# A fused attention and LoRA kernel: first loads laid out anew, cache rows fetched by GpSimd's indirect DMA, transposed keys from step 11

## The reference, cut to what matters

```python
q = einsum('bsd,ed->bse', x, Wq)   # 32 heads of 128
k = einsum('bsd,ed->bse', x, Wk)   # 8 heads of 128
v = einsum('bsd,ed->bse', x, Wv)
q = rope(rmsnorm(q, q_norm_w), cache_seqlens + arange(128))
k = rope(rmsnorm(k, k_norm_w), cache_seqlens + arange(128))
kc = k_cache[block_table].reshape(8, 512, 8, 128)   # 16 pages of 32 rows a sequence
vc = v_cache[block_table].reshape(8, 512, 8, 128)
k_all, v_all = concatenate([kc, k]), concatenate([vc, v])
scores = where(valid, q k_all^T / sqrt(128), -1e30)
x = x + (softmax(scores) @ v_all) @ Wo^T
x = x + linear with a LoRA; x = x + linear with 8 gated LoRA experts; x = x + SwiGLU with LoRAs
```

## Time and profile before

| | |
|---|---|
| median of 3 runs | 1474.0 us (1472.37 to 1478.88) |
| the profiled execution's own time | 1474.48 us |
| its span, first to last instruction | 1472.7 us |
| mean granted TensorE clock | 0.992 |
| attention, up to its last residual addition | about 1138 us |
| PE busy in the span | 1412.7 us (96%) |
| GpSimd (POOL) busy | 792.3 us (54%) |

### The profile page before, as it was taken

One profiled execution on the slowest core, in us unless ns is written; L12 is line 12 of the kernel. 1 busy time (PEld: TensorE's weight loads), 2 busy tenths in 40 slices (PEclk: granted clock), 3 DMA queues, 4 the chain that ended last, 5 costly groups with the idle time before them and its releaser, 6 DMA issues.

```text
span 1472.7 us, 27069 instructions
## 1 busy us (share of the span) xinstructions
PE 1412.7 (96%) x8052; PEld 1216.4 (83%) x8052; DVE 1113.9 (76%) x2236; ACT 852.8 (58%) x2082; POOL 792.3 (54%) x768
## 2 busy tenths in 40 slices
PE   2899999999999999999999999999997999899999
PEld 1788888888888888888888888888885777788887
DVE  4788888888888888888888888888886555554444
ACT  1666666666666767676676766666664322433332
POOL 5555555565555666666666666665551002454342
PEclk9999999999999999999999999999999899999999
DMA  4433333333333232223222222322425500334341
GB/s 125 152 111 105 107 104 102 102 108 105 113 100 104 69 81 66 65 65 75 68 67 65 65 78 62 70 55 47 116 43 164 113 1 1 110 118 118 118 117 66
DMA packets 192562, 129.68 MB, mean 88 GB/s; under 512 B 119041, under 2 KB 159745, under 8 KB 190113
## 3 DMA queue, kind: packets, MB, share of 16 engines
q1 hardware_dynamic: 192416, 127.96, 31.8%
HBM read 125.04 MB, written 24.64 MB: 102 GB/s over the span
## 4 chain that ended last, share of the span: by engine, by line
PE 81%; SPq 11%; issue 3%; DVE 3%; POOL 1%; DMA 1%; ACT 1%; DVEq 0%; POOLq 0%
PE banks L300 19%; PE banks L301 19%; PE banks L302 19%; PE banks L1207 10%; PE banks L1184 8%; SPq L346 5%; SPq L330 2%; SPq L354 2%; PE banks L1148 2%; DMA w_raw<-in_w_att 1%; PE banks L1376 1%; PE banks L1362 1%; PE banks L1254 1%; POOL w_pair L475 1%; PE banks L1302 1%
## 5 line engine op out<-in xcount | busy, mean ns | idle before, releaser
L651 ACT ACTIVATE prob<-prob,nbias 128x640 f32<-128x640 f32 x256 | 210.2, 822 | 151.9 <-DVE nbias L837 151.9
L812 DVE TENSOR_TENSOR pt_pair<-banks,pt_pair 128x640 fp32r<-128x640 f32 x256 | 211.0, 824 | 106.1 <-ACT pt_pair L647 103.6
L837 DVE CUSTOM_DVE_ANT_0 prob<-banks,mask,q_rs 128x640 f32<-128x640 f32 x256 | 220.2, 879 | 42.4 <-PE banks L302 42.4
L1207 PE MATMUL banks<-w_pair,o_pair 128*128 128x512 f32 x768 | 224.4, 414 | 2.1 <-DVE o_pair L812 2.1
L647 ACT ACTIVATE pt_pair<-banks 128x640 fp32r<-128x640 f32 x256 | 179.5, 701 | 42.8 <-PE banks L1184 42.8
L300 PE MATMUL banks<-w_pair,x_pair 128*128 128x256 f32 (+1 forms) x512 | 179.1, 350 | 21.4 <-POOL w_pair L475 21.4
L1184 PE MATMUL banks<-ident,prob 128*128 128x128 f32 x1280 | 184.2, 274 | 4.7 <-DVE pt_pair L812 4.7
L1184 PEld LDWEIGHTS banks<-ident,prob 128*128 128x128 f32 x1280 | 146.5, 140 | 47.3 <-issue 35.4
L301 PE MATMUL banks<-w_pair,x_pair 128*128 128x256 f32 (+1 forms) x512 | 174.1, 340 | 0.0
L302 PE MATMUL banks<-w_pair,x_pair 128*128 128x256 f32 (+1 forms) x512 | 173.4, 339 | 0.0
L300 PE MATMUL banks<-kt_pair,qt_pair 128*128 128x320 f32 x512 | 164.3, 321 | 2.5 <-DVE kt_pair L812 2.2
(11 more groups left out here) (188 smaller groups left out, 3488.0 us busy)
## 6 DMA issues: line engine op xcount, KB each, us to landing
w_raw<-in_w_att SPq DMA_DIRECT2D x64, 320.0 KB, 3.1
w_raw<-in_fw SPq DMA_DIRECT2D x66, 256.0 KB, 3.4
x_raw<-in_xT SPq DMA_DIRECT2D x64, 256.0 KB, 3.2
kt_all<-in_kT SPq DMA_DIRECT2D x128, 128.0 KB, 2.5
kv_raw<-in_kv SPq DMA_DIRECT2D x416, 32.0 KB, 1.6
kt_raw<-kt_all SPq DMA_DIRECT2D x38, 256.0 KB, 3.0
kv_raw<-in_kv SPq DMA_DIRECT2D x608, 16.0 KB, 1.6
fb_all<-in_gu_b SPq DMA_DIRECT2D x32, 176.0 KB
```

Of the source, the lines that this page charges most:

```text
L651: act.activation(prob[:, h, :], prob[:, h, :], ACT.Exp, bias=nbias[:, h:h + 1], scale=-1.0, accum_out=psum_row[:, h:h + 1]).then_inc(exped, 1)
L812: dve.tensor_tensor(pair[1], src, pair[0].bitcast(F32), ALU.subtract).then_inc(lo_sem, 1)
L837: dve.tensor_tensor_reduce(out=prob[:, h, :].rearrange("p (a n) -> p a n", a=2), in0=score_ps[h % 2][:, :, 0:HALF], in1=mask[:, n % B, :]. ...
L1207: last = pe.matmul(misc_ps, o_pair[:, j, h, :], w_pair[:, k, ds(at + h * HID, HID)], start=i == 0, stop=i == 3 * REP - 1)
```

## The change: what it does

1. **First loads.** The first group's weights come from an array of their own, `w_boot`, into a buffer `boot_raw` that holds all of them, in seven DMAs with a semaphore each: K and V columns first, then q's in four, then the output projection's 1 MB. `boot_raw` lies where `pt_pair` will be. VectorE makes high and low parts of x and of the first six itself; GpSimd makes the low part of the output projection's four. `tabs` are made for one sequence at a time: sequence 0 before step 0, then `make_tabs(n + 2)` at the end of VectorE's steps 0 to 5. Four instructions are made of eight. `w_att` pieces 0 to 7 are no longer loaded.
2. **Cache rows.** GpSimd computes row numbers once, and `load_rows(n + 2)` issues four indirect DMAs a step, each of 128 rows of 1 KB (K and V together, in all 64 steps). It stands behind `v_low(n)` and ahead of `kc_low(n+1)`. SP issues no cache rows.
3. **Transposed pages.** SP gathers all 16 pages of a sequence in each of steps 0 to 7, and `BY_ROWS` is 11: cached keys come by columns from step 11 on. SP waits once for all gathers.
4. ScalarE issues the loads of the page numbers, the first rotation rows, `wnorm` and `ident` at the start. The sign of the sine moves from the table to a subtraction.

The diff, cut to its core:

```diff
-BY_ROWS = 3 * B + 2
+BY_ROWS = B + 3
 # SP
+            def load_kt(n, par):
+                if n >= BY_ROWS + 2:
+                    sp.wait_ge(kc_lo, n - BY_ROWS - 1)
+                if n == BY_ROWS:
+                    sp.wait_ge(s_gathered, 16 * NPP * B)
+                    sp.wait_ge(tab_done, B)
+                sp.dma_start(kt_raw[:, par, :]..., kt_all[n % B, :, n // B]...).then_inc(s_ktin[par], 16)
+            def gather_keys(b):
                 _, pages = nc.values_load_multi_w_load_instructions(...)
                 for j, page in enumerate(pages):
-                    a = PSIZE * (j % 4)
-                    sp.dma_start(kv_raw[a:a + PSIZE, par, j // 4, at:2 * D], t["kv"][...]).then_inc(s_kvin[par], 16)
-                if 2 <= n < BY_ROWS:
-                    gather_keys(b, pages, (n - 2) // B)
+                    sp.dma_start(kt_all[b, j]..., t["kT"][ds(page), :, :]...).then_inc(s_gathered, 16)
             load_x(0, 0)
-            load_w(0, 0)
-            load_w(1, 1)
+            for j, (lo, hi) in enumerate(BOOT_COLS):
+                sp.dma_start(boot_raw[:, lo:hi], t["w_boot"][:, lo:hi]).then_inc(s_boot[j], 16)
+            load_x(1, 1)
...
+            sp.dma_start(boot_raw[:, WWO:GW], t["w_boot"][:, WWO:GW]).then_inc(s_boot[len(BOOT_COLS)], 16)
             def step(n, par, x=True, w=True):
...
-                load_kv(n + 2, par, True)
+                if n < B:
+                    gather_keys(n)
+                if n + 2 >= BY_ROWS:
+                    load_kt(n + 2, par)
 # GpSimd
+            def load_rows(n, par):
+                if n >= 2:
+                    pool.wait_ge(v_lo, n - 1)
+                    pool.wait_ge(kt_done, n - 1)
+                for c in range(KC - 1):
+                    pool.indirect_dma_start(kv_raw[:, par, c, :], None, t["kv"],
+                                            bass.IndirectOffsetOnAxis(ap=row_at[:, n % B, c:c + 1], axis=0),
+                                            element_offset=(n // B) * PAGES * PSIZE * 2 * D).then_inc(s_kvin[par], 16)
...
                 v_low(n, par)
+                if n + 2 < NT:
+                    load_rows(n + 2, par)
                 if nxt and n + 1 >= BY_ROWS:
                     kc_low(n + 1, 1 - par)
-                if isinstance(n, int) and n == 0:
-                    w_low(PIECES - 1, 1)
                 if x:
                     x_low(n + 2, par)
                 if w:
                     w_low(n + PIECES, par)
 # VectorE, before step 0
+            def boot_split(j):
+                lo, hi = BOOT_COLS[j]
+                dve.wait_ge(s_boot[j], 16)
+                dve.tensor_scalar(w_pair[:, 0, lo:hi], boot_raw[:, lo:hi], 1.0, None, ALU.mult).then_inc(boot_hi, 1)
+                dve.wait_ge(boot_hi, j + 2)
+                dve.tensor_tensor(w_pair[:, 1, lo:hi], boot_raw[:, lo:hi], w_pair[:, 0, lo:hi].bitcast(F32),
+                                  ALU.subtract).then_inc(boot_lo, 1)
+            for j in range(len(BOOT_COLS)):
+                boot_split(j)
+            make_tabs(0)
+            dve.wait_ge(s_boot[len(BOOT_COLS)], 16)
+            for j in range(REP):
+                lo, hi = WWO + j * HID, WWO + (j + 1) * HID
+                dve.tensor_scalar(w_pair[:, 0, lo:hi], boot_raw[:, lo:hi], 1.0, None, ALU.mult).then_inc(boot_out_hi, 1)
+            q_times_cos(0)
...
+            k_rope(0, 0)
+            qt_low(0)
+            kt_low(0)
 # VectorE, end of a step
+                if n + 2 < B:
+                    make_tabs(n + 2)
 # TensorE
-            pe.wait_ge(s_const, 48)
             project_kv(0, 0)
             project_q(0, 0)
+            pe.wait_ge(s_const, 16)
```

More of the change, by code:

```diff
@@ L48 @@
 QKV_PIECES = -(-WWO // PW)
+BOOT_COLS = [(WKV, WKV + HID), (WKV + HID, WWO)] + [(j * HID, (j + 1) * HID) for j in range(DC)]
 POS_END = 1645
@@ L112, in build @@
         qt_pair = sb("qt_pair", [P, 2, REP, P], F32R, where=att)
+        boot_raw = sb("boot_raw", [P, GW], where=boot)
+        boot.close()
         pt_pair = sb("pt_pair", [P, 2, REP, KC, P], F32R, where=att)
@@ L239, in build @@
         kt_hi, kt_lo = sem("kt_hi"), sem("kt_lo")
-        s_gathered = [sem(f"s_gathered{b}") for b in range(B)]
+        s_gathered = sem("s_gathered")
+        s_page, page_step, rows_known = sem("s_page"), sem("page_step"), sem("rows_known")
         s_ktin = [sem(f"s_ktin{i}") for i in range(2)]
@@ L676, in step @@
                 pt_high(n, 2)
-            x_high(0, 0)
+            act.wait_ge(added, 1)
+            for j in range(KC - 1):
+                act.dma_start(page_i[j * PSIZE:(j + 1) * PSIZE].rearrange("p b c -> p (b c)"),
+                              t["pages_by_place"][j].partition_broadcast(PSIZE)).then_inc(s_page, 16)
+            act.dma_start(in_page[:, 0:1], t["in_page"]).then_inc(s_page, 16)
+            act.activation(spare[:, 0:1], spare[:, 2:3], ACT.Copy)
+            _, first_length = nc.values_load_multi_w_load_instructions(
+                t["seqlens"].unsqueeze(0)[:, 0:1], engines=[act.engine], min_val=0, max_val=POS_END - 1,
+                skip_runtime_bounds_check_because="cache lengths are below POS_END")
+            load_trig(act, 0, first_length[0], s_trig0)
+            act.dma_start(wnorm[:], t["wnorm"].partition_broadcast(P)).then_inc(s_trig0, 16)
+            act.dma_start(ident[:], t["ident"]).then_inc(s_const, 16)
             copy_kv(0, 0)
@@ L865, in add_attention @@
                 dve.tensor_tensor(dst, misc_ps, dst, ALU.add).then_inc(added, 1)
-            for m in range(QKV_PIECES):
-                w_high(m, m % 2)
-            dve.wait_ge(s_trig, 16 * (B + 1))
-            h = D // 2
[L872 to L877, removed]
-                        out=tabs[:, :, 2 * k + tab, half], in0=src, scalar=sign * scale,
-                        in1=wnorm[:, k, half].unsqueeze(1).broadcast_to([P, B, h]), op0=ALU.mult, op1=ALU.mult)
@@ L880, in _, with make_tabs @@
-            last.then_inc(tab_done, 1)
-            w_high(QKV_PIECES, QKV_PIECES % 2)
-            dve.wait_ge(s_const, 48)
+            def make_tabs(b):
+                if b == 0:
+                    dve.wait_ge(s_trig0, 32)
+                elif b == 1:
+                    dve.wait_ge(s_trig1, 16)
+                elif b == 2:
+                    dve.wait_ge(s_trig, 16 * (B - 2))
+                h = D // 2
+                for k in range(2):
+                    scale = -1.0 if k == 0 else float(D) ** 0.5
+                    for j in range(2):
+                        last = dve.scalar_tensor_tensor(
+                            out=tabs[:, b, 2 * k + j, :].rearrange("p (a d) -> p a d", a=2),
+                            in0=trig[:, b, j * h:(j + 1) * h].unsqueeze(1).broadcast_to([P, 2, h]), scalar=scale,
+                            in1=wnorm[:, k, :].rearrange("p (a d) -> p a d", a=2), op0=ALU.mult, op1=ALU.mult)
+                last.then_inc(tab_done, 1)
@@ L1122, in project_q @@
             def project_q(n, par):
-                if not (isinstance(n, int) and n == 0):
+                if n:
                     pe.wait_ge(qt_lo, n)
```

165 lines of the change are left out of this document (93 added, 72 removed).

## The result

| | before | changed |
|---|---|---|
| median | 1474.69 us (4 runs, 1472.37 to 1478.88) | 1791.2 us (4 runs, 1789.5 to 1792.94) |
| ratio, 95% interval | | 1.2141 (1.2122 to 1.216) |
| span of the profiled execution | 1472.7 us | 1790.3 us |
| mean granted TensorE clock | 0.992 | 0.923 |

The kernel is 21% slower; 8.7% was forecast, with 1718 us as the upper end. The direction and the place were right, the size was not. Executions of one kernel differ by up to 0.6% (1472.4 to 1481.8 us for the kernel before, over all its runs), so a smaller difference between kernels that were run once is read only from the length of their steps.

What follows compares the result with a forecast made beforehand. TensorE was taken to bound the kernel, with SP binding early; from step 11 GpSimd's DMA loop would bind. 1474.5 + 140.4 - 4 + 3 - 11.5 = 1602.4, median 1602 us; range 1498 to 1718.

Steps and rivals of the forecast that it cites:

- The mechanism: From step 11, TensorE's next scores wait for `kc_low`, which waits behind four indirect DMAs on GpSimd: +140.4 us.
- the period of 15.6 + 4d with d = 1.0: Steps 11 to 62: loop of 15.6 us plus four indirect DMAs of d us each, giving 19.6 us a step.
- the lower bound: Least d for one indirect DMA: 0.5 us, from SP's plain row loads at 0.55 with their registers.
- Nothing in the loop shrinks with the wait: Loop through `kc_low`: its parts keep their times while TensorE waits; only the slack ahead of `k_norm` changes.
- Steps 1 to 10: DMAs fit GpSimd's idle time, so steps fall from 17.64 to 17.18 us: -4 us, against +3 for `make_tabs`.
- a step of room: `x_low` and `w_low`, queued behind the DMAs on GpSimd, were said to have this slack; `kc_low` only 1.2 us.
- if the cover is gone: Early steps: without VectorE's some 2 us free a step, `make_tabs` costs some 12 us instead of +3.
- Start: Before step 0's attention: first loads no longer held back, first mask and min near 26.4 us: -11.5 us.
- After step 62: The stretch from step 62 to the end; nothing was forecast to change after attention: 0.
- The cheap indirect DMA: Rival: an indirect DMA costs GpSimd next to nothing, under 0.29 us; loop stays under 16.77, total 1455 us; chance 0.12.
- The rival that VectorE holds up GpSimd's DMAs: Three of four DMAs wait half a microsecond for VectorE: period 21.1 us, total 1680 us; chance 0.13.
- SP did not bind in the early steps: Answers a rival: SP or the DMA engines bind in steps 0 to 7, adding 35 us, total 1637; chance 0.05.

Runs made afterwards that it cites:

- the filler: Changed kernel plus 18 TensorE matmuls of 512 columns, their results unused, in each step's wait for `kc_low`: 1701.8 us.
- the rows last: Changed kernel with the four indirect DMAs moved from ahead of `kc_low` to the end of GpSimd's step, behind `w_low`: 1508.3 us.

## Why the prediction was wrong

**The mechanism was right.** The loop through `kc_low`, with its 52 intervals, is where 303 of the 318 us are, and each edit that takes DMAs out of the loop takes time out too, as the order alone changes: four in the loop 22.7 us a step, two 18.5, none 17.6.

**The failed step is the period of 15.6 + 4d with d = 1.0, and what it leaves out.** The measured period is 22.73. It is made of 15.55 for the loop (the 15.39 of the trace before, and 0.15 from `kc_low`'s end at 905.19 to the scores at 905.34), 5.16 for the DMAs, and 2.0 that are left, of which the filler shows 1.8 to be the clock.

- *Size of d.* Busy time is 0.95 to 1.10, close to the 1.0 taken from the rows nearest to it. But 0.28 to 0.30 us of idle time stands ahead of each, and four cost 5.16. I priced an instruction and not its pitch, although the lower bound beside it was made from a pitch. It is +1.1 us a step, 58 us. d with its gap is 1.29, inside the range of 0.5 to 1.56, so this alone would have left the time inside the range. The Trainium skill ("DMA: Bandwidth & Descriptors", Latency and other measured facts) gives about 1 us for the first byte on the GpSimd path. That figure lies near the busy time of 0.95, but it is a latency and does not say how long GpSimd's queue is held; no run here shows the latency by itself.
- *"Nothing in the loop shrinks with the wait."* True, but something grows: "TensorE's projection, which comes a fixed time behind the scores" is not fixed. After its wait of 3.9 us TensorE runs its next matmuls at the lower level (granted clock 0.50 from 906 to 908), and these are in the loop. The prediction put this term at nothing. It is +2.0 us a step, 105 us, the largest part of the miss, and it took the result out of the range. The filler shows most of it: with 18 matmuls more a step the 52 steps take 20.94 us each, 1.8 less; the other 0.2 stays open.
- *Steps 1 to 10.* Forecast -1, measured +18.2. `x_low` was said to have a step of room; it has 2.3 us against 5.16, and that makes 18.4 us a step in steps 6 to 10. `make_tabs` was given 0.5 us; it costs 2.1 because pushed GpSimd work falls on it. The 12 us that the prediction named "if the cover is gone" was the right size, but it came from that order and not from VectorE's spare time.
- *Start.* Forecast -11.5. The first mask and min stands at 27.69 instead of 37.95, -10.3, of which step 0 loses 3 before the first marker; why was not tried.
- *After step 62.* Forecast 0, measured +3.4, which comes and goes with the granted clock there (0.97 or 0.98) in kernels without the DMAs too.

In the order of size of d, clock, steps 1 to 10, start and end, the misses are 58 + 105 + 19 + 4 + 3 = 189 us, the distance from 1602 to 1791.

**The rivals.** The cheap indirect DMA did not come. The rival that VectorE holds up GpSimd's DMAs asked for 1.5 us a step and did not come at that size: the mean of a DMA is 0.99 us against a least one of 0.94, so 0.2 us a step, and with the rows last the median is 1.03 against 0.95. It was VectorE that waited, for GpSimd's two-input instructions. SP did not bind in the early steps: from step 1 to 10 of the changed kernel its queue waited 69.5 us for `w_low`, and TensorE waited for no DMA there.

## What to carry to other kernels

An engine's idle share says nothing on whether work can be put there: look in its order at the gap between the place of the new work and the next instruction that another engine waits for, and do so for each instruction that is pushed, not for the first alone. Here the kernel was 317 us slower than before with the four instructions in one place and 34 with them in another, and from step 11 on TensorE was full once SP fetched the rows. When a change makes TensorE wait for some microseconds in each step, price the wait and then also the matmuls behind it at half the clock. Price an instruction by its pitch, from start to start, and not by its duration.

## What the runs showed of the hardware

- An indirect DMA of 128 rows holds GpSimd for 0.95 us, 1.10 for the first of a series, with 0.30 between two, for rows of 512 bytes and of 1 KB alike.
- TensorE's mean granted clock was 0.90 where it waited 3.9 us in each step of 22.7, 0.95 where it waited 2.5 in steps of 20.5, 0.99 where it waited 1.4 in steps of 18.5, and 1.0 when matmuls without use filled the wait. After one wait the clock was 0.50 for at least two microseconds of matmuls.
- A VectorE instruction with two inputs in SBUF waited up to 3.5 us behind two GpSimd instructions in a row, and ran at its usual 0.28 beside GpSimd's indirect DMAs.
